# Attention block and frequency-split convolution on one core: the maximum pass spaced, the kept blocks' exponentials one unit earlier, and the next image's scale waited for where it is used

## The reference, cut to what matters

```python
q, k, v = Wq @ xf, Wk @ xf, Wv @ xf              # 32, 32 and 256 channels, n pixels
attn = softmax((q.T @ k) / sqrt(32), axis=-1)    # n x n for every image
x    = gamma * (Wo @ (v @ attn.T)) + x
low  = mean over 2x2 pixels of x
high = x - upsample(low)
low  = prelu(bn(mag_w @ low + mag_b))
high = prelu(bn(phase_w @ [high, high rolled by one row] + phase_b))[:256]
out  = upsample(low) + high                      # rows rolled inside patches of 8 x 8
```

## Time and profile before

| | us |
|---|---|
| runs | 2339.72, 2341.36, 2341.66 |
| median | 2341.36 |
| the profiled execution, its own time | 2340.45 |
| its span, first to last instruction | 2338.5 |
| PE busy | 2205.9 (94%) |
| PE weight load busy | 1764.1 (75%) |
| DVE busy | 1782.4 (76%) |
| ACT busy | 1431.6 (61%) |
| POOL busy | 677.7 (29%) |

### The profile page before, as it was taken

One profiled execution on the slowest core, in us unless ns is written; L12 is line 12 of the kernel. 1 busy time (PEld: TensorE's weight loads), 2 busy tenths in 40 slices (PEclk: granted clock), 3 DMA queues, 4 the chain that ended last, 5 costly groups with the idle time before them and its releaser, 6 DMA issues.

```text
span 2338.5 us, 48099 instructions
## 1 busy us (share of the span) xinstructions
PE 2205.9 (94%) x16373; PEld 1764.1 (75%) x16373; DVE 1782.4 (76%) x3388; ACT 1431.6 (61%) x2547; POOL 677.7 (29%) x891
## 2 busy tenths in 40 slices
PE   5799999999989999999998999999999999999997
PEld 4577777777767777777777777777777777777776
DVE  6777877777867788877786877777877777778764
ACT  3457666657656666666656666566665656666663
POOL 3232332232322323322232321323322232233321
PEclk8799999999999999999999999999999999999998
DMA  4254444454554444444474443443445444344443
GB/s 159 59 115 94 99 109 102 84 117 99 135 131 85 110 107 92 109 108 97 93 168 102 99 99 72 104 96 91 103 111 133 75 89 93 77 82 88 84 86 64
DMA packets 596617, 235.02 MB, mean 101 GB/s; under 512 B 547072, under 2 KB 548352, under 8 KB 596576
## 3 DMA queue, kind: packets, MB, share of 16 engines
q1 hardware_dynamic: 596576, 234.51, 45.5%
HBM read 67.67 MB, written 32.53 MB: 43 GB/s over the span
## 4 chain that ended last, share of the span: by engine, by line
PE 64%; DVE 15%; issue 10%; DMA 5%; ACT 3%; POOL 1%; SPq 1%; DVEq 0%; ACTq 0%; POOLq 0%
PE M L482 13%; PE M L519 7%; PE O L631 7%; PE O L633 6%; PE O L632 6%; PE O L644 6%; PE O L646 6%; PE O L645 6%; DVE pq L1052 5%; DMA pt<-pq 4%; PE S L590 4%; DVE saved L947 4%; DVE pmax L943 2%; DVE pl L1047 2%; PE M L500 1%
## 5 line engine op out<-in xcount | busy, mean ns | idle before, releaser
L758 ACT ACTIVATE ph<-S 128x512 f16<-128x512 f32 x512 | 307.6, 601 | 525.5 <-PE S L590 524.8
L644 PE MATMUL O<-uh,pt 128*128 128x257 f16 x2048 | 568.2, 277 | 16.9 <-DMA pt<-pq 16.7
L631 PE MATMUL O<-uh,ph 128*128 128x257 f16 x2048 | 570.3, 278 | 4.5 <-DVE pl L1047 4.1
L633 PE MATMUL O<-uh,pl 128*128 128x257 f16 x2048 | 563.2, 275 | 0.0
L632 PE MATMUL O<-ul,ph 128*128 128x256 f16 x2048 | 561.8, 274 | 0.0
L646 PE MATMUL O<-uh,pt 128*128 128x257 f16 x2048 | 559.0, 273 | 0.0
L645 PE MATMUL O<-ul,pt 128*128 128x256 f16 x2048 | 555.7, 271 | 0.0
L947 DVE TENSOR_SCALAR_CACHE_REDUCE saved<-M 128x512 f32<-128x512 f32 x512 | 344.0, 687 | 257.0 <-PE M L519 253.0
L1047 DVE TENSOR_TENSOR pl<-p,ph 128x512 f16<-128x512 f32 x512 | 402.6, 787 | 60.5 <-ACT p L761 59.1
L519 PE MATMUL M<-kst,qst 96*128 (+1 forms) x1024 | 424.0, 442 | 20.9 <-DVE saved L947 16.2
L1052 DVE TENSOR_TENSOR pq<-saved,pq 128x512 f16<-128x512 f32 x512 | 387.6, 757 | 19.2 <-ACT saved L770 19.1
(11 more groups left out here) (161 smaller groups left out, 2907.4 us busy)
## 6 DMA issues: line engine op xcount, KB each, us to landing
xr<-in_x SPq DMA_DIRECT2D x53, 512.0 KB, 3.8
out_y<-z SPq DMA_DIRECT2D x33, 512.0 KB, 3.0
xb<-in_x SPq DMA_DIRECT2D x25, 512.0 KB, 3.7
pt<-pq SPq DMA_TRANSPOSE x512, 3.1
qraw<-q_scratch SPq DMA_DIRECT2D x99, 64.0 KB, 2.0
uh_scratch<-uh_next SPq DMA_DIRECT2D x24, 257.0 KB, 3.2
uh<-uh_scratch SPq DMA_DIRECT2D x24, 257.0 KB, 3.2
ul_scratch<-ul_next SPq DMA_DIRECT2D x24, 256.0 KB, 3.1
```

Source lines behind the costliest of these rows:

```text
L631: nc.tensor.matmul(O[j][:, 0:UW], ph[:, i % 4, q], uh[:, i, :], start=(i == 0), stop=False)
L633: ins = nc.tensor.matmul(O[j][:, 0:UW], pl[:, i % 4, q], uh[:, i, :], start=False, stop=False)
L644: nc.tensor.matmul(O[j][:, 0:UW], pt[:, k % RING, i, :], uh[:, t, :], start=False, stop=False)
```

## The change

Five edits. The list `DOUBLE` of units with two maxima is another one. `EXP_AT` of all slots is one unit earlier; `LOW_AT` is one unit earlier for the first ten slots and the same for the others. The scan moves from unit 20 to 22, the copy of the queries from 27 to 28. On SP the transpose of slot 2 goes ahead of the output's store. The scale: VectorE does only the small reduction of maxima before the image, and the rest of `find_scale` in unit 0 of the image's first turn, after `normalise`; ScalarE waits for `scaled` at the first "u" task. For this an image's first turn is written out ahead of the loop on VectorE.

```diff
-ROUND_X, ROUND_CONV, SCAN, NEGATIVE, QUERIES = 9, 14, 20, 26, 27
+ROUND_X, ROUND_CONV, SCAN, NEGATIVE, QUERIES = 9, 14, 22, 26, 28
-DOUBLE = (11, 13, 15, 16, 18, 25)
+DOUBLE = (9, 13, 17, 22, 24, 26)
-EXP_AT = [AT["k", k] - 5 for k in range(NK)]
-LOW_AT = [AT["k", k] - (3 if k < ND - RISE else 4) for k in range(NK)]
+EXP_AT = [AT["k", k] - 6 for k in range(NK)]
+LOW_AT = [AT["k", k] - 4 for k in range(NK)]
@@ turns
-                    with eng.Fori(0, inner) as c:
+                    if image_start:
+                        image_start(pair_i * 2 + parity, pair_i * (2 * NCH) + parity * NCH, parity, scans=True)
+                    with eng.Fori(begin, inner) as c:
@@ SP, turn
+                turn_slot(g, 2)
                 sp.wait_ge(out_ready, g + 1)
                 gp = (g + (ALL - 2)) % ALL
                 sp.dma_start(out_v[ds(gp // NCH, 1), ds(gp % NCH, 1)], z[:, :, :]).then_inc(out_stored, 16)
-                turn_slot(g, 2)
@@ ScalarE, take
                 elif kind == "u":
+                    if task[1] == 0:
+                        act.wait_ge(scaled, g // NCH + 2)
                     act.wait_ge(u_stored, 32 * g + 32)
-            def before_image(image, parity):
-                act.wait_ge(scaled, image + 2)
@@ VectorE
+            def bound_x(parity):
+                nc.vector.tensor_reduce(bnd[:, 0:1], amax[:, parity, :], AX.X, ALU.max).then_inc(bound, 1)
             def find_scale(image, parity):
-                nc.vector.tensor_reduce(bnd[:, 0:1], amax[:, parity, :], AX.X, ALU.max).then_inc(bound, 1)
                 dve.wait_ge(reduced, image + 1)
@@ VectorE, turn
                     if t == (0 if plan is FULL else 1):
                         normalise(g)
+                    if t == 0 and scale_of is not None:
+                        find_scale(scale_of + 1, 1 - parity)
@@ VectorE, before_image
                 dve.wait_ge(xs_scanned, image * NCH + 1)
-                find_scale(image + 1, 1 - parity)
-            turns(dve, turn, before_image)
+                bound_x(1 - parity)
+            turns(dve, turn, before_image,
+                  image_start=lambda image, g, parity, scans: turn(g, parity, 0, FULL, scans, scale_of=image))
```

More of the change, by code:

```diff
@@ L254, in kind_of, with turns @@
             return [task for task in plan.number if task[0] == kind]
-        def turns(eng, turn, before_image=None, before_last=None, image_end=None):
-            inner = NCH - 1 if image_end else NCH
+        def turns(eng, turn, before_image=None, before_last=None, image_start=None, image_end=None):
+            begin, inner = (1 if image_start else 0), (NCH - 1 if image_end else NCH)
             with eng.Fori(0, B // 2 - 1) as pair_i:
@@ L270, in turns @@
                 before_image(B - 2, 0)
-            with eng.Fori(0, inner) as c:
+            if image_start:
+                image_start(B - 2, (B - 2) * NCH, 0, scans=False)
+            with eng.Fori(begin, inner) as c:
                 turn((B - 2) * NCH + c, 0, c, FULL, scans=False)
@@ L839, in turn @@
                         round_conv(g)
-            def before_image(image, parity):
-                act.wait_ge(scaled, image + 2)
-            turns(act, turn, before_image)
+            turns(act, turn)
             copy_out(ALL, 0)
@@ L921, in _ @@
             dve.wait_ge(scanned0, NCH)
+            bound_x(0)
             find_scale(0, 0)
@@ L1037, in normalise @@
                 dve.wait_ge(rs_step, 2 * g + 1)
-                gain = ogain[:, B - 1:B] if isinstance(g, int) else ogain[:, ds((g + (ALL - 1)) % ALL // NCH, 1)]
+                gain = ogain[:, ds((g + (ALL - 1)) % ALL // NCH, 1)]
                 nc.vector.tensor_tensor(rs[:, :], rs[:, :], gain.to_broadcast([128, SUB]), ALU.mult).then_inc(rs_step, 1)
@@ L1100, in finish_chunk, with turn @@
                 finish_q(M[1], g + 2, m_free[1])
-            def turn(g, parity, c, plan, scans):
+            def turn(g, parity, c, plan, scans, scale_of=None):
                 if plan is not FULL:
```

## The result

The changed kernel takes 2355.69 us in the median of 4 runs (2354.29 to 2357.54), the kernel before 2341.51 (2339.72 to 2342.63, 4 runs). The ratio is 1.0063, 95% interval 1.0047 to 1.0079: slower by 0.6%. Forecast were 2354 us and slower. The profiled execution took 2354.49 us, its span 2352.7.

The account below looks back on a forecast made before the run. TensorE's own order of work was taken as the bound, 64% of the chain of waits. Ordinary turns +19, first turns -18.6, last image +11, final turn +1 gave +12.6: about 2354 us, 0.5% slower; 8-in-10 range 2336 to 2367.

Parts of the forecast that it names:

- Second maximum behind a convolution: Units 22 and 24: second maximum waits until ScalarE empties the convolution's bank; 0.87 and 0.88 us lost, 31 turns, 54 us.
- Start of the turn: Earlier exponentials and low halves of slots 0 and 1 delay tile 4's scores matmul (S4) 0.50 us, tile 4 0.89 more.
- rival 1: Units 0 to 4 have slack and absorb both exponential pairs: 40 us less, 2314; chance 0.12 faster, 0.13 within noise.
- Slot 2's transpose: TensorE's wait for slot 2's transposed copy goes entirely: 0.57 us in an ordinary turn, 1.3 to 2.8 in first turns.
- Maxima spaced: Bank waits before maxima of units 13 and 17, and a small one in unit 5, go: 1.14 us; last image 0.33.
- Queries' copy: Copy after the last maximum readies negated maxima 0.87 us earlier; gains 0.52 an ordinary turn, 0.85 in the last image.
- The thin cover: Turn's end: finished queries come about 0.2 us before TensorE asks for them; if gone, up to 0.3 a turn.
- First turns: Turns 0, 8 and 16: scale ready sooner, tile 4's scores matmul earlier; -8.3, -5.8, -4.5, together -18.6 us.
- the reduction starts as before: First turns: GpSimd's partition reduction keeps its start, so the scale still comes 7.1 us after turn 8's begin.
- the clock: First turns: assumed not to fall after the 3 us idle left; otherwise up to 3 us come back in each.
- Rival 3, the port: First turns: reduction holds the shared port, VectorE's tile 0 low half waits; 3, 3 and 2 us, 2362; chance 0.08.
- Rival 4: VectorE falls behind more than reckoned, units 7 to 12 and turn's end: 0.3 more a turn, +9, 2363; chance 0.13.

Follow-up runs that it names:

- the fastest kernel: Changed kernel with maxima pairs moved to units 19 and 23, slot 11's exponentials one unit later, slots 0 and 1 in their old units: 2245.70 us, ratio 0.9599.

## Why the prediction was right, step by step

| term | forecast | in the two traces |
|---|---|---|
| 21 ordinary turns | +19 | +19.3 |
| 3 first turns | -18.6 | -15.4 |
| 7 turns of the last image | +11 | +12.3 |
| final turn | +1 | +0.1 |
| before the first and after the last turn | 0 | -2.2 |
| sum | +12.6 | +14.2 |

The forecast's terms add up to 12.5, not 12.6; that changes nothing.

**Second maximum behind a convolution**: forecast 0.87 and 0.88 us. In the changed trace the second maximum starts 0.90 and 0.87 later than its pace, on average over all 31 turns. What the forecast left out is the matmul behind it, another 0.10 each: together 1.97 us a turn and 61 us in all, where 1.75 and 54 stood in the sum. The mechanism is shown from both sides: moving the pairs away takes 61.7 us off, putting them alone onto the kernel before adds 50.2.

**Start of the turn**: 0.50 and 0.89 forecast, together 1.39; in turn 13 S4 comes 0.47 later and tile 4 1.37 later in all. The experiment with only the first two slots shows it: it gives back 28 us. In the last image the start costs more than the 1.0 forecast, some 1.2: there the first maximum, too, waits for the low part of the next queries, which VectorE takes behind normalise (4.7 us in 7 waits, a row that the kernel before doesn't have). The forecast's sum holds, but its rival 1 was priced wrongly: it said that without these waits 40 us would go. With the lead kept for the other slots it is 28 to 30; with the lead undone for all it is 2.

**Slot 2's transpose**: the wait went, as forecast, but the part of the order on SP in it was not, as it may seem, nothing: beside an on-time start it is worth 11.0 us. That the late start covers it in the changed kernel is likely but wasn't run. I credited the lead and the order with one wait and did not part them.

**Maxima spaced**: -1.14 was the sum of the waits of units 5, 13 and 17, and in the changed kernel none of them is left. The spacing alone doesn't do it: put alone onto the kernel before, it leaves weight loads waiting 35.7 us for maxima. Nor does it take the late start: with slots 0 and 1 in their old units and the others' lead kept, the start is on time and these waits stay away.

**Queries' copy**: 0.52 and 0.85 forecast, together 18 us; undoing it cost 20.5. The thin cover held: no new wait for the finished queries appears (one of 2.4 us in both kernels). In the last image the gain was 0.71.

**First turns**: here a term was mis-sized, by 3.2 us together. In turn 0 the forecast -8.3 met -8.4. Turns 8 and 16 gained 4.5 and 2.5 instead of 5.8 and 4.5. (By the sum turn 16 would have taken 71.4 us, not the 72 to 73 of the prediction's last paragraph.) Two assumptions failed, and they made up more than the difference; 0.8 to 0.9 us in each of the two turns came back, since the later S4 hid the wait for tile 4 that the sum had counted. First, that the reduction starts as before: GpSimd adds up the outputs of the turn before it, and against the turn's begin it is done later now. In turn 8, which begins at 660.25, the timeline of GpSimd in the changed kernel:

```profile
660.17 0.20 POOL L1201 TENSOR_TENSOR bndspare<-bnd 128x1 f32<-128x1 f32 x1
666.62 0.38 POOL L1202 PARTITION_ALL_REDUCE bndall<-bnd  x1 [6.24 <-issue]
```

And of TensorE, S4 and S5:

```profile
669.73 0.49 PE L594 MATMUL S<-qcur,kst 128*128 128x512 f32 x1 [3.38 <-ACT p L765]
...
674.35 0.48 PE L594 MATMUL S<-qcur,kst 128*128 128x512 f32 x1
```

The result is there 6.75 us after the begin instead of 6.2; in turn 16, which begins at 1229.16 and where GpSimd stood 5.96 us before its result against 5.52, 6.0 against 4.7. S4 comes 9.48 and 8.75 after the begin, not 8.9 and 7.3. Second, the clock: behind 3.38 and 2.65 us of idle time in turns 8 and 16 the granted clock stood at 1.2 GHz again for a while. Busy time of the changed kernel in short stretches behind the S4 of turn 8 and of turn 16, and at the start of turn 13:

```profile
669.80:673.00 3.20, 3.20 (x19) 2.79 (x19) 1.98 (x3) 3.20 (x7) 0.00 (x0) 0.68 0.00 0
...
1238.40:1241.00 2.60, 2.60 (x13) 2.48 (x12) 1.56 (x3) 2.60 (x6) 0.00 (x0) 0.51 0.00 0
1020.00:1023.00 3.00, 2.90 (x25) 2.22 (x23) 2.72 (x7) 2.95 (x7) 0.00 (x0) 1.00 0.09 22
```

The granted clock is 0.68 and 0.51 of full speed there against 1.00. From S4 to S5 it takes 4.62 and 4.36 us, against 3.00 in turn 13. The prediction named this case and put up to 3 us on each first turn. Whether it happens is in part luck: the same start in other kernels of this case went either way. Behind 2.36 us of idle time the clock was down in the kernel with only the first two slots put back, and behind 3.03 us it stayed up in the fastest kernel. Busy time behind the S4 of turn 16, first the one, then the other:

```profile
1223.30:1226.30 3.00, 3.00 (x17) 2.71 (x18) 1.96 (x3) 3.00 (x7) 0.00 (x0) 0.66 0.00 0
...
1177.00:1179.90 2.90, 2.90 (x25) 2.73 (x26) 1.98 (x3) 2.90 (x6) 0.00 (x0) 1.00 0.00 0
```

**Rival 3, the port**: false. VectorE's first low half of turn 8 ran beside the reduction, at its ordinary length, and so did those of turns 0 and 16. GpSimd's idle time before its result was 6.24 us against 6.59 before in turn 8, 5.96 against 5.52 in turn 16: no clear difference. The timeline of VectorE in the changed kernel:

```profile
661.33 0.69 DVE L1054 TENSOR_TENSOR pl<-p,ph 128x512 f16<-128x512 f32 x1 [0.93 <-ACT p L765]
```

So the reduction does not hold the port all the while. The Trainium skill (SBUF — State Buffer, section "Who interferes with whom") has the contention only for a GpSimd instruction that reads SBUF; what the reduction does in those 6 us, this trace doesn't show. Beside GpSimd's elementwise work the low halves do take up to 1.26 us, as before (1.22).

**Rival 4**: an ordinary turn came out at +0.92 us on average against the +0.91 of the sum; the 0.3 more a turn did not come. That the two numbers agree so closely is luck in part. Averaged over the ordinary turns, the start costs 1.37 us as forecast and the banks 1.97 instead of 1.75; the waits between unit 4 and the convolutions give back 1.87 instead of 1.71 (two fewer maxima there taken into account), and the turn's end 0.55 instead of 0.52.

**Left open**: why, with the lead undone, the late copies and the bank waits of units 9 to 17 add up to almost exactly what the start gave. Open, too, is why the final turn's +1 didn't come.

## What to carry to other kernels

When tasks alternate between two banks, the second task behind a long one waits for the long one's eviction, whichever engine runs it: put at most one short task behind it before other work. A unit of lead moved to all items of an in-order queue is not free: the first items land in front of the evictions that everything else waits for, so give the lead only to the items that were late. And a cost found in one place can't be taken off as a gain by undoing its cause as a whole: here the same edit held a cost of 28 to 30 us and a gain of nearly as much, and only splitting it by slot told them apart.

## What the runs showed of the hardware that was not expected

TensorE's granted clock was down behind the 2.65 us of idle time of turn 16, where I had assumed that it would stay up. The length of the idle time alone doesn't settle it: at the same place the clock was down behind 2.36 us in one kernel and up behind 3.03 us in another. A matmul that follows one which had to wait for its bank starts 0.34 us after it, instead of 0.24. GpSimd shows 5.5 to 6.6 us of idle time before the result of a reduction over partitions of three columns, in every image of both traces, with no quicker later ones, and VectorE's two-operand instruction beside it takes its ordinary 0.69 us.
